# The loop over the two middle batches of an attention layer, written out on every engine

## What is computed

```python
def attn(x):                        # 32 heads of 16, 8 key/value heads
    q, k, v = x @ Wq.T, x @ Wk.T, x @ Wv.T
    q, k = rope(q), rope(k)
    p = softmax(causal(q @ k.T / 4))          # per head, 512 x 512
    return (p @ v) @ Wo.T

def ffn(x):                         # 512 -> 1792 -> 512
    W1, W2, W3 = (m + mean(abs(w - m)) * sign(w - m) for w, m in ...)
    return (silu(x @ W1.T) * (x @ W3.T)) @ W2.T

x = layernorm(x + attn(x))
x = layernorm(x + ffn(x))
```

## Time and profile before

| | us |
|---|---|
| median of 3 runs | 1021.18 |
| lowest and highest | 1018.03 and 1021.41 |
| the profiled execution's own time | 1019.75 |
| its span, first to last instruction | 1018.0 |

### The profile page before, as it was taken

One profiled execution on the slowest core, in us unless ns is written; L12 is line 12 of the kernel. 1 busy time (PEld: TensorE's weight loads), 2 busy tenths in 40 slices (PEclk: granted clock), 3 DMA queues, 4 the chain that ended last, 5 costly groups with the idle time before them and its releaser, 6 DMA issues.

```text
span 1018.0 us, 17370 instructions
## 1 busy us (share of the span) xinstructions
PE 928.5 (91%) x5698; PEld 642.8 (63%) x5698; DVE 708.8 (70%) x1223; ACT 359.4 (35%) x681; POOL 258.9 (25%) x323
## 2 busy tenths in 40 slices
PE   4389979899798999999888899999999999999994
PEld 2244535455354554555467788888888888888883
DVE  7587756666566566765459577778777877778777
ACT  1026646655566556564753011111111111111124
POOL 2046434654246442321223101110111001110000
PEclk9579999999899999999899899999999999999997
DMA  4746766744357432331342001111011101110004
GB/s 171 103 151 163 219 180 199 183 143 132 102 164 175 138 106 74 91 77 44 106 164 74 3 2 61 62 62 61 1 62 62 62 9 52 62 62 1 1 0 166
DMA packets 49700, 95.41 MB, mean 94 GB/s; under 512 B 11424, under 2 KB 25760, under 8 KB 48608
## 3 DMA queue, kind: packets, MB, share of 16 engines
q1 hardware_dynamic: 49632, 94.53, 31.8%
HBM read 66.72 MB, written 14.02 MB: 79 GB/s over the span
## 4 chain that ended last, share of the span: by engine, by line
PE 73%; DVE 8%; issue 6%; POOL 5%; DMA 3%; ACT 3%; SPq 2%; POOLq 0%; ACTq 0%; DVEq 0%
PE PS L967 18%; PE PS L969 17%; PE PS L968 17%; PE PS L1082 6%; PE PS L1054 5%; PE PS L1072 5%; PE PS L1074 2%; PE PS L1056 2%; DVE negM L820 2%; POOL xL L499 1%; DMA Qs<-parts 1%; POOL co L504 1%; ACT Pt L611 1%; SPq L351 1%; POOL rp L487 1%
## 5 line engine op out<-in xcount | busy, mean ns | idle before, releaser
L820 DVE TENSOR_REDUCE negM<-PS 128x1 f32<-128x384 f32 (+3 forms) x352 | 217.3, 637 | 136.4 <-PE PS L1056 134.9
L611 ACT ACTIVATE Pt<-PS 128x512 f32<-128x512 f32 (+1 forms) x352 | 194.2, 561 | 167.3 <-PE PS L1074 131.9
L967 PE MATMUL PS<-XH,WH 128*128 128x512 f32 x448 | 176.1, 393 | 3.8 <-DVE XL L776 3.8
L968 PE MATMUL PS<-XL,WH 128*128 128x512 f32 x448 | 175.3, 391 | 0.0
L969 PE MATMUL PS<-XH,WL 128*128 128x512 f32 x448 | 175.3, 391 | 0.0
L564 ACT ACTIVATE sg<-PS 128x512 f32<-128x512 f32 x56 | 33.6, 601 | 383.0 <-PE PS L969 383.0
L1054 PE MATMUL PS<-Ks,Qs 96*128 96x384 bf16 (+3 forms) x512 | 144.4, 315 | 25.4 <-DMA Qs<-parts 14.8
L1072 PE MATMUL PS<-Qs,Ks 99*128 99x256 bf16 (+3 forms) x512 | 141.1, 309 | 17.9 <-ACT Pt L611 13.3
L726 DVE TENSOR_TENSOR y<-PS,y 128x512 f32<-128x512 f32 x224 | 138.7, 683 | 0.0
L471 POOL TENSOR_TENSOR Wr<-Wr 128x512 f32<-128x512 f32 x42 | 54.5, 1326 | 318.5 <-DMA Wr<-wall 318.5
L1054 PEld LDWEIGHTS PS<-Ks,Qs 96*128 96x128 bf16 x512 | 51.2, 101 | 121.0 <-DVE negM L820 66.9
(11 more groups left out here) (101 smaller groups left out, 1292.5 us busy)
## 6 DMA issues: line engine op xcount, KB each, us to landing
co<-wall SPq DMA_DIRECT2D x42, 512.0 KB, 5.1
Wr<-wall SPq DMA_DIRECT2D x42, 512.0 KB, 4.2
Qs<-parts SPq DMA_DIRECT2D x96, 128.0 KB, 3.8
o_dram<-Oe SPq DMA_DIRECT2D x32, 256.0 KB, 2.4
xraw<-xt SPq DMA_DIRECT2D x16, 256.0 KB, 3.9
Oc<-o_dram SPq DMA_DIRECT2D x16, 256.0 KB
y<-x SPq DMA_DIRECT2D x4, 1024.0 KB, 7.6
Inv<-inv_dram SPq DMA_DIRECT2D x16, 256.0 KB
```

Of the source, the lines that this page charges most:

```text
L611: act.activation(Pt[:, t % 2, h:h + m, P * t:S], PS[:, BANK_P2 + (g[1] * NU + n) % 2, 0:m * w].rearrange("p (m w) -> p m w", m=m), ACT.Exp ...
L820: dve.tensor_reduce(negM[:, g[1] % 2, h:h + m, t], PS[:, BANKS_P1[(g[1] * NU + n) % 3], 0:m * w].rearrange("p (m w) -> p m w", m=m), AX_X, ...
L967: pe.matmul(dst, stH, moH, start=(k == 0), stop=False)
L968: pe.matmul(dst, stH, moL, start=False, stop=False)
```

## The change

The loop over `b` in `sections` becomes a loop at build time, so that each engine's program holds the code of section 1 and behind it that of section 2, with constants in all their waits and addresses. `hold` keeps its wait, but adds to `passed` only where the awaited value is a register's; after the change that is left in SP's feed-forward loop alone. So the increments go in sections 0, 3 and 4 and in the transfers ahead of section 0 too.

```diff
     eng.wait_ge(semaphore, value)
-    eng.sem_inc(passed, 1)
+    if not isinstance(value, int):
+        eng.sem_inc(passed, 1)
...
                 run.section(Section(0, False, True, True))
-                with run.eng.Fori(1, B - 1) as b:
+                for b in range(1, B - 1):
                     run.section(Section(b, True, True, True))
                 run.section(Section(B - 1, True, True, False))
```

## The result

The changed kernel takes 1008.2 us (median of four runs, 1007.08 to 1013.19); the kernel before, run beside it, 1020.24. The ratio is 0.9895 with a 95% interval of 0.9862 to 0.9927, so the change saves 7.4 to 14.1 us, 10.7 in the middle. The forecast was a saving of 8.3 us and 1012.9 us.

What follows compares the result with a forecast made beforehand. PE was taken as the busiest engine, idle some 20 us in the looped sections. Edge 5.69, SP's train 2.0, POOL 0.45 and entry 0.2 sum to 8.3 us: 1021.18 to 1012.9 us, range 1008.5 to 1018.0.

Steps and rivals of the forecast that it cites:

- The edge, 5.69 us: Between sections 1 and 2: without PE's branch back, its 3.79 us gap and 1.90 us of half clock go.
- the control: Passage from section 2 to 3, same PE work with the branch not taken: 13.82 us against 19.51 at the edge.
- PE and ACT run on into straight code: Between sections 1 and 2: with the branch gone, both engines continue as from section 0 into 1 and 2 into 3.
- so I expect no drop at the edge either: Between sections 1 and 2: PE's clock stays at 1.00 after its 1.69 us wait for ACT; 3.79 us if it falls.
- SP's train, 2.0 us: Sections 1 and 2: shorter gaps between SP's transfers let PE start about 1.0 us earlier in each step 3.
- Half clock in step 3: Rival, 0.10: step 3's stall no longer lowers PE's clock, 1.65 us back each time, 11.6 us saved, 1009.6.
- the sum: Whole kernel: 5.69 + 2.0 + 0.45 + 0.2 = 8.3 us saved.
- POOL, 0.45 us: Split of the maxima: fewer increments on POOL shorten five PE waits by 0.09 us each, between 0 and 0.85.
- the entry, 0.2: Start of section 1: PE's 4.54 us wait for the transposed maxima shortens some 0.2 us, or nothing.
- The branch was the cause: Against the rival, 0.08, that PE's branch holds up nothing: edge worth 0.1 us, whole change 2.7 us, 1018.5.
- nothing new waited at the edge: Against the rival, 0.14, that the stall moves: half of 5.69 us comes back, 4.5 us saved, 1016.7.
- the feed-forward turns: Rival, 0.04: feed-forward loop stops being resident, four turns cost 22.8 us, kernel 14.5 us slower, 1035.7.

## Why the prediction was right, and where not

**The edge, 5.69 us.** Right in size and mechanism: 5.77 us by the passages (19.51 - 13.74), a clock of 1.00 in the five microseconds at the edge, and the 1.75 us wait for ACT left, as the control said. What I had only half seen is that ACT's stall was a second, equal cause: "PE and ACT run on into straight code" holds, but the change would have been worth nothing at the edge with either loop left.

Less safe than I wrote is "so I expect no drop at the edge either". It came true in the changed kernel, but with the increments kept the clock fell at an edge that is just as straight, and the passage took 14.87 us. The control scatters the same way: over the thirteen kernels with the full work the passage from section 2 to 3 took 13.73 to 13.82 us in seven and 14.88 to 14.91 in six, and in those six the granted clock fell to 0.50 behind the wait of about 1.7 us. So about 1.1 of the 5.77 us hangs on a clock that falls in one execution and not in another.

**SP's train, 2.0 us.** This step failed: it took the gaps that registers and increments make between SP's transfers for what sets PE's wait. The gaps shrank as forecast (`o_dram` 0.73 us earlier), and counted from the wide product the third part went out 1.21 and 0.97 us earlier, as forecast too. But it landed only 0.61 and 0.76 us earlier, since it took longer to land (6.4 us in section 1 against 5.8, a contention that I had put at nothing), and the waits fell by 0.45 and 0.61, 1.06 instead of 2.0. SP straight alone kept waits of 2.33 and 1.77 us, only 0.07 and 0.44 less than before, while SP looped with PE and ACT straight had 1.05 and 1.09, 1.35 and 1.12 less. What sets the wait is the landing of the third part, and ahead of it that of the `o_dram` write. In the kernel before a packet of PE's code ran into that write, and its last part landed 1.32 and 0.93 us behind the others. In section 1 of the changed kernel no packet did, and yet the write took 3.8 us, where it took 2.7 with PE and ACT alone written out; the reason stays open.

**Half clock in step 3.** I gave it 0.10 as a rival, and half of it came: section 1 has a clock of 1.00 in the 3.30 us behind the wait, section 2 still 0.57. The two steps around step 3 together were shorter by 2.29 us in section 1 and 0.96 in section 2. Of the 2.29, PE's idle places explain 0.99: 0.45 for ACT, 0.19 and 1.20 for the two waits for POOL, less a new wait of 0.85 for the transposed maxima. The remaining 1.3 us are near the 1.65 that the rival had worked out for the clock. In section 2 the idle places explain 0.75 of the 0.96. So the sum was near by a compensation: less from the wait, more from POOL and the clock. That the clock stayed up in section 1 was luck, as far as these runs show: it did so behind a wait of 1.95 us, while without the feed-forward loops it was 0.53 in the 3.30 us from 192.5 on, behind a wait of 1.02.

**POOL, 0.45 us, and the entry, 0.2.** Before section 1's and 2's step 3 the wait fell from 0.92 to 0.73 and 0.74 us, twice the estimated 0.09; with the increments kept it was 0.85 in both, so about 0.12 of the 0.19 goes with them. The second such wait went from 1.20 to under 0.1 in section 1, where the wait for the maxima came instead, and from 0.87 to 0.90 in section 2. The wait at the entry fell from 4.54 to 3.32, but the passage there only from 17.8 to 17.5 us, near the 0.2 of the sum: the granted clock over that passage was 0.90 before and 0.80 after.

**The rivals that didn't happen.** The branch was the cause; nothing new waited at the edge; the feed-forward turns stayed at 0.2 us. Steps stayed at 12.52.

**The size.** Forecast 8.3 us, 8.83 in the attention by the profile, 10.7 by the medians (7.4 to 14.1). The interval holds all three. That the raw median fell 0.3 us outside the range is within what the feed-forward part scatters, 3 us; the profiled run, the slowest, had a granted clock of 0.959 over its span, the others 0.962 to 0.966. Whether the last 2 us have a cause beyond that stays open. Moving the loads further gave nothing measurable, and the best median measured here, 1006.25 us with only PE and ACT written out, can't be told from the changed kernel.

## What to carry to other kernels

Look for the branch back of a run-time loop in the sequencer's rows, and price the edge by a passage with the same work and no branch taken; then check every engine whose first instruction after the branch comes late, since a stall behind another is paid in full when only one is removed. Read that passage in several executions, since the granted clock alone moved it by 1.1 us here. Writing out the loop of the engines that stall is enough; register waits cost nothing where the work ahead covers them. What a shorter train of issues gains can't be told until it is known which landing ends the wait.

## What the runs showed of the hardware

- The price of the same taken branch on PE was 3.930 us in the kernel before, 4.275 with SP straight, 6.209 with two blocks of 512 KB sent 0.4 us ahead of its start and 0.1 us behind it, 3.869 with these sent later, 0.243 with a body 512 instructions shorter (one execution each). Its end came 1.40 to 1.44 us after the end of a 16 KB packet of code, so what varied was when that packet ran: it started 1.2, 1.7, 3.8 and 1.5 us after the branch.
- ACT lost 4.30 to 5.14 us at its edge with a body of 323 traced instructions, while DVE, with 290, went on 0.3 us after its branch (branch at 251.1, next loop instruction at 251.4, in the kernel with the short body).
- PE's code came in single packets of 16 KB, in a queue of its own beside the data's. One took 0.9 to 2.1 us in these traces, and in the ten cases where one started in the first 1.3 us of the `o_dram` write of 256 KB, the last of that write's sixteen parts landed 0.9 to 1.6 us after the one before it. In nine of the other ten cases that was 0.04 to 0.4 us, in one 1.1.
